# A two-block transformer kernel: top-k search one tile earlier, second block's weight split moved, last results in banks of their own

## The reference, cut to what matters

```python
# attention 1: 16 heads of 64, softmax over the 77 keys, then Wo, bo
x = x + tanh(g_xattn[1]) * attention1(layernorm(x), ctx)
# feed-forward 1: each expert chooses its tokens
n = layernorm(x)                                   # [4, 1024, 256]
affinity = softmax(n @ gate_w.T)                   # [4, 1024, 8]
gating, idx = top_k(affinity.transpose(0, 2, 1), 256)   # 256 tokens a batch and expert
h   = silu(n[idx] @ w_gate.T) * (n[idx] @ w_up.T)  # 1024 wide
x_e = h @ w_down.T
x = x + tanh(g_ffn[1]) * scatter_add(idx, gating * x_e)
```

## Time and profile before

| what | us |
|---|---|
| median of the runs shown | 1408.33 |
| the profiled execution | 1407.95 |
| its span (first to last instruction) | 1406.2 |
| PE busy in the span | 1297.4 (92%) |
| DVE, ACT, POOL busy | 911.0, 761.5, 627.0 |
| mean granted TensorE clock, of full speed | 0.945 |
| attention 1 | about 556 to 858 |
| feed-forward 1 | about 857 to 1406 |

### The profile page before, as it was taken

The page is one execution under the profiler, slowest core; times in us unless marked ns, Lnnn a source line. Parts: engine busy times, 40 slices in busy tenths (PEclk is TensorE's granted clock), DMA queues, the critical chain, the costliest instruction groups (busy, mean ns, idle before and its releaser), DMA issues.

```text
span 1406.2 us, 29217 instructions
## 1 busy us (share of the span) xinstructions
PE 1297.4 (92%) x9858; PEld 975.7 (69%) x9859; DVE 911.0 (65%) x2128; ACT 761.5 (54%) x2315; POOL 627.0 (45%) x664
## 2 busy tenths in 40 slices
PE   7966699999999999899999985899999999999997
PEld 3755588879999968788888773356656666566555
DVE  2887664565555577778776885777776555566651
ACT  3775332432332365988887752655645555555551
POOL 2177678666666540454444433133333333333113
PEclk8675599999999999999999996999999999999999
DMA  4657444654334351100210103244444444444322
GB/s 146 213 163 184 96 50 56 122 109 67 63 60 64 63 142 40 39 32 32 91 39 24 34 31 93 106 120 121 121 121 124 150 158 148 126 130 129 108 45 31
DMA packets 81546, 133.17 MB, mean 95 GB/s; under 512 B 24662, under 2 KB 71260, under 8 KB 76316
## 3 DMA queue, kind: packets, MB, share of 16 engines
q1 hardware_dynamic: 51132, 93.92, 20.1%
q0 software_dynamic: 29312, 37.57, 16.5%
q10 hardware_dynamic: 992, 0.27, 0.1%
HBM read 95.08 MB, written 36.65 MB: 94 GB/s over the span
## 4 chain that ended last, share of the span: by engine, by line
PE 70%; DVE 10%; DMA 6%; issue 5%; POOL 5%; ACT 2%; SPq 0%; POOLq 0%; ACTq 0%; DVEq 0%
PE psG L124 5%; PE psG L126 5%; PE psG L125 5%; PE psU L124 5%; PE psU L126 5%; PE psU L125 5%; PE psYb L124 4%; PE psYb L125 4%; PE psYb L126 4%; DMA stage<-in_w 3%; PE psP L1798 2%; PE psS L124 2%; PE psS L125 2%; PE psS L126 2%; PE psOL L126 2%
## 5 line engine op out<-in xcount | busy, mean ns | idle before, releaser
L2118 POOL DMA_INDIRECT out_x<-yo,gidx x64 | 100.2, 1566 | 324.0 <-ACT yo L2220 310.8
L2268 DVE SCALAR_TENSOR_TENSOR hid<-psU,sil 128x512 f32<-128x512 f32 x128 | 88.4, 691 | 167.2 <-ACT sil L2209 166.7
L980 POOL DMA_INDIRECT x_rows<-yo,tabs x78 | 124.7, 1599 | 91.7 <-ACT yo L1052 68.0
L1720 ACT ACTIVATE pr<-psS,mx 128x77 f32<-128x77 f32 x512 | 158.8, 359 | 5.2 <-DVE mx L1889 5.2
L2209 ACT ACTIVATE sil<-psG 128x512 f32<-128x512 f32 x128 | 76.4, 597 | 118.1 <-PE psU L126 118.1
L126 PE MATMUL psYb<-W1dh,hl 128*128 128x256 f16 x512 | 139.6, 273 | 0.0
L125 PE MATMUL psYb<-W1dl,hh 128*128 128x256 f16 x512 | 139.6, 273 | 0.0
L124 PE MATMUL psYb<-W1dh,hh 128*128 128x256 f16 x512 | 139.6, 273 | 0.0
L1079 DVE SCALAR_TENSOR_TENSOR hid<-psU,sil 128x512 f32<-128x512 f32 x78 | 53.8, 690 | 127.3 <-ACT sil L1043 127.2
L1720 ACT ACTIVATION_READ_ACCUMULATOR pr<-psS,mx 128x1 f32 x512 | 123.6, 242 | 0.0
L1043 ACT ACTIVATE sil<-psG 128x512 f32<-128x512 f32 x78 | 46.5, 596 | 134.2 <-PE psU L126 132.2
(11 more groups left out here) (407 smaller groups left out, 4331.1 us busy)
## 6 DMA issues: line engine op xcount, KB each, us to landing
w1u<-in_w SPq DMA_DIRECT2D x16, 2048.0 KB, 7.4
w1d<-in_w SPq DMA_DIRECT2D x16, 1024.0 KB, 9.7
stage<-in_w SPq DMA_DIRECT2D x8, 1536.0 KB, 8.9
X<-in_x SPq DMA_DIRECT2D x8, 512.0 KB, 8.6
n_rows<-xc SPq DMA_DIRECT2D x8, 512.0 KB, 9.0
x_rows<-X SPq DMA_DIRECT2D x8, 512.0 KB, 10.2
X<-x_rows SPq DMA_DIRECT2D x8, 512.0 KB, 8.0
out_x<-X SPq DMA_DIRECT2D x32, 128.0 KB, 1.7
```

The costliest lines, as they stand in the source:

```text
L980: pool.indirect_dma_start(x1_rows[:, :], bass.IndirectOffsetOnAxis(tabs[:, j, n, 0:1], 0), yo[:, par, n, :], None, compute_op=ALU.add).the ...
L1720: ins = act.activation(pr1[:, par, h * LK:(h + 1) * LK], psS1[:, q, i * LK:(i + 1) * LK], ACT.Exp, bias=mx1[:, h:h + 1], scale=1.0 / (SX * ...
L2118: pool.indirect_dma_start(out_rows[:, :], bass.IndirectOffsetOnAxis(gidx[:, half, col:col + 1], 0), yo1[:, j % 2, n, :], None, compute_op= ...
L2268: dve.scalar_tensor_tensor(hid1[:, f % 2, :], psU1[f % 2][:], SH / (SX * SW), sil1[:, f % 2, :], ALU.mult, ALU.mult).then_inc(d_hid, 1)
```

## The change

1. The first half's search stands one tile earlier: softmax at t == 18 (soft_max no longer ahead of that step's residual, but after probs_low0), rows at 22 to 24, digits from 26, THR in scores0 of tile 31, RANKS on PE in step 32 instead of 34 and in bank 3 of psS1 (so it needs exps1 of the last tile only).
2. The one-hot halves of the first half (4 on DVE) are placed singly between the last tiles' probs and statistics. The other two, the product with the token number, go to ACT as eight Copies with a scale (`values_act`), and FILL waits for them. TURN on PE stands before the last tile's transposes.
3. Block 1's up weights are split behind attention 1, in topk_scalar and topk_vector (eight pieces each), no longer in block 0's step.
4. The second half's row transposes stand in block 0's up (after f = 1 to 4), its first count at f = 7, and so do block 1's transposes (after f = 3), rows_high (f = 5) and rows_low (f = 6). The transposes signal for each k. gates_sync(1) goes behind load_down(1) on SP.
5. The pieces of the up weights are split in the order 0, 2, 4, 6, 1, 3, 5, 7, and `up` waits for four pieces at f = 0 and for the rest at f = 4.
6. The last block's four results go to four banks (two of psYb, two of psXb), each signalled and copied singly.

```diff
+        UP_PIECES = (0, 2, 4, 6, 1, 3, 5, 7)
-        drain0, drain1 = psS1[:, 0, :], psS1[:, 1, :]
-        FIRST_DIGIT = 27
-        ROWS_AT = ((0, 23), (1, 24), (0, 24), (1, 25))
-        FIRST_ODD = 25
-        TAIL_PE = {(27, "a"): THR, (28, "a"): RANKS, (29, "b"): FILL, (30, "b"): TURN}
-        TAIL_DVE = {(27, "a"): THR, (28, "b"): RANKS, (29, "b"): FILL, (30, "b"): TURN}
+        drain0, drain1 = psS1[:, 0, :], psS1[:, 3, :]
+        FIRST_DIGIT = 26
+        ROWS_AT = ((0, 22), (1, 23), (0, 23), (1, 24))
+        FIRST_ODD = 24
+        HOT = TURN + 1
+        TAIL_PE = {(26, "b"): RANKS, (29, "b"): FILL, (29, "d"): TURN}
+        TAIL_DVE = {(27, "a"): (RANKS,), (27, "d"): (HOT,), (27, "b"): (HOT + 1,), (28, "c"): (HOT + 2,),
+                    (28, "a"): (HOT + 3,), (29, "b"): (FILL,), (30, "b"): (TURN,)}
...
+            if t == FIRST_DIGIT + DIGITS // 2:
+                return THR
...
+        PE_ORDER = [("transposes_out", 5), ("turn2", 3), ("tail_a", 6), ("outputs0", 3), ("tail_c", 6), ("transposes_in", 0), ("scores0", 1),
+                    ("outputs1", 3), ("turn0", 2), ("outputs2", 3), ("turn1", 2), ("digit_odd", 3), ("scores1", 0), ("tail_b", 6), ("logits", 6), ("tail_d", 6)]
+        ACT_ORDER = [("exps1", 2), ("probs_high0", 3), ("shares_exp", 5), ("exps0", 2), ("probs_high1", 3), ("values", 5), ("copy_out", 5),
+                     ("high_in", 0), ("weights_high", 0), ("shares_copy", 5), ("probs_high2", 3)]
+        DVE_ORDER = [("stats_in", 0), ("normalise_out", 6), ("tail_c", 7), ("moments_in", 0), ("residual", 5), ("digit_odd", 5), ("probs_low0", 4), ("shares_max", 5),
+                     ("count_odd", 5), ("tail_a", 7), ("stats_out", 5), ("moments_out", 5), ("largest1", 2), ("reciprocals", 3), ("probs_low1", 4),
+                     ("maxima1", 2), ("low_in", 1), ("tail_d", 7), ("probs_low2", 4), ("largest0", 2), ("digit", 2), ("maxima0", 2),
+                     ("shares_div", 5), ("count", 2), ("normalise_in", 0), ("tables", 0), ("weights_low", 2), ("tail_b", 7)]
...
+        def values_act(act):
+            for half in range(2):
+                act.wait_ge(k_dve, D_MASK + 4 + 3 + half)
+                for i in range(half * (NI // 2), (half + 1) * (NI // 2)):
+                    row = hotC[:, i * RB:(i + 1) * RB, :]
+                    ins = act.activation(row, row, ACT.Copy, scale=tokv[:, i:i + 1])
+                ins.then_inc(k_act, 1)
...
         def topk_scalar(act):
+            for f in range(FT1 // 2):
+                second_high(act, f)
             soft_exp(act, 1)
             copies_act(act, 1)
-            for n in range(ROWS):
-                rows_act(act, 1, n, psYb[:, n, :].rearrange("p (k n) -> p k n", k=2))
-            gates_act(act, 1)
+            for f in range(FT1 // 2, FT1):
+                second_high(act, f)
...
             soft_div(dve, second, 1)
-            count(dve, second, 1, 0)
+            for f in range(FT1):
+                cols = slice(UP_PIECES[f] * UC, (UP_PIECES[f] + 1) * UC)
+                dve.wait_ge(d_wh, FT1 + f + 1)
+                dve.scalar_tensor_tensor(W1ul[1][:, cols], w1u[:, cols], SW, W1uh[1][:, cols],
+                                         ALU.mult, ALU.subtract).then_inc(d_wl, 1)
...
                 load_down(sp, j)
+                if j == 1:
+                    gates_sync(sp, 1)
...
                 pe.wait_ge(d_xl, KD * j + KD)
-                pe.wait_ge(d_wl, FT1 * j + FT1)
                 for f in range(FT1):
+                    if f % (FT1 // 2) == 0:
+                        pe.wait_ge(d_wl, FT1 * j + FT1 // 2 + f)
...
+                    if j == 0 and 1 <= f < 1 + ROWS:
+                        rows_pe(pe, 1, f - 1, [psYb[:, f - 1, k * P:(k + 1) * P] for k in range(2)])
+                    if j == 0 and f == 3:
+                        transposes(1, 1)
...
+        def result(j, n):
+            if j == NB1 - 1:
+                return (psYb[:, 0, :], psYb[:, 2, :], psXb[:, 0, 0:D], psXb[:, 1, 0:D])[n]
+            return psYb[:, n, :]
...
-            pipeline(pe, NB1, DD, [(2, up), (1, transposes), (3, down)], unroll=4, straight=True)
+            pipeline(pe, NB1, DD, [(2, up), (1, next_transposes), (3, down)], unroll=4, straight=True)
```

More of the change, by code:

```diff
@@ L1807, in run @@
                         wait(pe, c_res, t)
+                    if n == 0 and t == 19:
+                        pe.wait_ge(k_dve, 1)
                     if t == 0 and n == 2:
@@ L1819, in run @@
                         return
-                    for n in range(2):
-                        pe.wait_ge(c_exp[n], T)
+                    pe.wait_ge(c_exp[1], T)
+                    if TAIL_PE[t, name] != RANKS:
+                        pe.wait_ge(c_exp[0], T)
                     choose_pe(pe, 0, TAIL_PE[t, name], drain0, drain1)
@@ L1931, in counts @@
                     count(dve, ch, 0, 0)
-                if even_of(t) is not None:
+                if even_of(t) is not None and even_of(t) != THR:
                     count(dve, ch, 0, even_of(t) + 1)
@@ L1946, in run @@
                         return
-                    p = TAIL_DVE[t, name]
-                    choose_dve(dve, ch, 0, p, drain0, drain1)
-                    if p == RANKS:
-                        for n in range(6):
-                            one_hot_half(dve, ch, n)
+                    for p in TAIL_DVE[t, name]:
+                        if p >= HOT:
+                            one_hot_half(dve, ch, p - HOT)
+                        else:
+                            choose_dve(dve, ch, 0, p, drain0, drain1)
                 return run
@@ L2124, in ffn1_tensor, with next_transposes @@
         def ffn1_tensor(pe):
+            def next_transposes(j, ph):
+                if j != 1:
+                    transposes(j, ph)
             def transposes(j, ph):
@@ L2178, in run @@
                     par = ph % 2
-                    if isinstance(j, int) and j == 0:
+                    if j < 2:
                         return
@@ L2229, in hidden_high, with first_step, run, next_rows @@
                 return run
+            def first_step(f):
+                def run(j, ph):
+                    n = {2: 0, 3: 1, 4: 2, 6: 3}.get(f)
+                    if j == 0 and n is not None:
+                        rows_act(act, 1, n, psYb[:, n, :].rearrange("p (k n) -> p k n", k=2))
+                    if j == 0 and f == 5:
+                        rows_high(1, 1)
+                    if j == 0 and f == 7:
+                        gates_act(act, 1)
+                return run
+            def next_rows(j, ph):
+                if j != 1:
+                    rows_high(j, ph)
             work = [(2, silu(0)), (1, up_high(0)), (2, down_high(0))]
             for f in range(1, FT1):
-                work += [(2, silu(f)), (2, hidden_high(f - 1)), (1, up_high(f)), (2, down_high(f))]
-            work += [(2, hidden_high(FT1 - 1)), (1, rows_high)]
+                work += [(2, silu(f)), (2, hidden_high(f - 1)), (1, up_high(f)), (2, down_high(f)), (2, first_step(f))]
+            work += [(2, hidden_high(FT1 - 1)), (1, next_rows)]
             pipeline(act, NB1, DD, work + [(3, results)], unroll=4, straight=True)
```

115 lines of the change are left out of this document (65 added, 50 removed).

## The result

The changed kernel takes 1397.47 us (median of four runs, 1394.96 to 1399.40); the kernel before, run beside it, 1408.84 (1406.64 to 1411.07). The ratio is 0.9917, 95% interval 0.9901 to 0.9933: by it 11.7 us faster (9.4 to 13.9; the two medians as they stand differ by 11.4). The forecast was 1395.9 with a range of 1391.5 to 1401.5.

The account below looks back on a forecast made before the run. PE was taken as full in the steady blocks, so only its waits (attention 1's drain, between blocks 0 and 1, in block 1) could shrink: -8.0 - 2.8 - 1.3 = -12.1 from 1407.95 gives 1395.9 us, range 1391.5 to 1401.5.

Parts of the forecast that it names:

- Search a tile earlier: Attention 1's last tiles: a digit step moved earlier costs about +0.9 us, regained next step; taken as 0, bounds -1 to +1.
- One-hot halves singly: Drain of attention 1: last residual no longer behind the halves, -5.9 us, and -0.7 for THR; bounds -7.5 to -3.5.
- rival 1: Drain of attention 1: one-hot halves and pn shut each other out, last outputs 2 us later, 1397.9 us; chance 0.14.
- Residual to gather: Last residual to first gather: faster FILL (-0.9) and TURN no longer behind waiting transposes (-0.5), together -1.4 us, bounds 0 to -2.
- Gather to up(0): First gather to block 0's up: 11.26 us as before, with the same slow clock; no gain.
- Rows, transposes and splits inside up(0): From up(0) to up(1): 24.3 us instead of 27.1, so -2.8 us, bounds -3.2 to -1.
- Block 1's first three f: Start of block 1: its down weights bind, PE still waits 1.4 us; -1.3 us, bounds -2.7 and +4.3.
- Split behind attention hides: After attention 1: block 1's split, 4.9 us on DVE, ends some 2 us before rows_low(0); up to +3 if uncovered.
- Last results in own banks: Kernel end: block 14's scatter landing and four POOL scatters set the pace; 0, bounds -0.5 to +0.3 us.
- Rival 2: Block 1: down weights take 10.6 us, as behind a w1u; +5.6 and 1.7 for the clock, 1403.2 us; chance 0.10.
- Rival 3: Drain of attention 1: not DVE's alone, only half of the 8.0 us up to the gather comes, 1399.9 us; chance 0.11.
- Rival 4: Block 0: TensorE stays at 1.2 GHz throughout, +19 us gives 1415, slower than before; chance 0.03.

Follow-up runs that it names:

- e9: Changed kernel with digit numbers in PSUM, looser waits of the last scatters, block 0's down pieces by two, softmax at tile 19; ratio to the kernel before 0.9875.
- e4: Changed kernel with the two digit numbers that the one-hot halves compare in PSUM instead of SBUF; 1393.32 us, ratio to the kernel before 0.9895.
- e3: Changed kernel with the last block's results in pairs again, as before the change; ratio to the kernel before 0.9935.
- e5: Changed kernel with block 2's up weights loaded only when block 1's down weights are, so the loads pair again; 1410.57 us, ratio to the kernel before 0.9988.
- e11: Changed kernel with block 1's up weights split inside block 0's step again, all else kept; ratio to the kernel before 0.9979.
- e2: Kernel before with only parts 3 to 6 of the change, the old drain of attention 1 kept; 1404.95 us, ratio to the kernel before 0.9962.
- e10: Changed kernel with up weights split in plain order and up waiting for all eight pieces; ratio to the kernel before 0.9935.
- e1: Kernel before with only parts 1 and 2 of the change, feed-forward 1 as before; 1405.15 us, ratio to the kernel before 0.9964.

## Why the prediction was right, and where its terms were wrong

- **What bounds the kernel.** Right: the time came from the places where PE waited, and the steady blocks gave nothing (478.92 and 478.91 us).
- **Search a tile earlier, taken as 0.** It cost 1.00, the upper bound. The residual of tile 28 comes 2.29 us late (243.65 for 241.36), and tile 29's step gives only 1.29 of it back (7.94 for 9.23). The step with the softmax takes 11.05 us in place of 10.19; with the softmax back at tile 19, e9 is 0.64 faster.
- **One-hot halves singly: 6.6 forecast, 3.73 measured.** This is the step that failed. Of the missing 2.9, 1.00 is the search's, as above; behind tile 29 the drain gave 4.73. The working let the four halves stand in time in which DVE waited, and left pn at its 1.91. The halves did stand there, but the one beside pn stretched it, and PE's outputs of the last tile went back with it. e4 gives 1.64 back by removing just this: from tile 29 to the last residual it takes 14.21 us, a gain of 6.39 of the 6.6; 0.2 stay unexplained. So the 6.6 were worked out rightly but for pn. It is rival 1, priced at 2 us and given 0.14. It should have been in the sum: the row of a normalise taking 2.00 beside pn was there. Two of the prediction's own signs of being wrong came with it or behind it: pn and a half of over 1.5 us, and an end of down(15) to end of the kernel that is shorter than before (9.5 us for 10.4).
- **Residual to gather: 1.4 forecast, 2.37 measured.** Right in kind, too small. FILL took 1.06 for 1.91 as worked out, but also started 0.61 sooner behind the residual, since the logits and transposes ahead of it ran at full clock too; and TURN, standing free, gave 0.90 and not 0.5. The gather came at a distance of 272.44, 1.9 behind the 270.5 that the forecast's 8.0 makes of 278.54.
- **Gather to up(0), taken as 0: 0.41 gained.** PE's wait for the split rows fell from 2.08 to 1.41. It is not shown to be the change's: with the same code there, e3 to e9 took 10.86 to 11.39 us, beside 10.85 after and 11.26 before.
- **Rows, transposes and splits inside up(0): 2.8 forecast, 2.05 measured.** The work of up(0) came out as worked out, 24.1 us (25.07 less the wait) for 24.3, with the clock back at the same point as before. What was missed is the 0.96 us for which PE still waits for gxl ahead of up(1).
- **Block 1's first three f: 1.3 forecast, 2.41 measured.** The chain was right link by link. From up(0)'s end (886.19 - 0.96 = 885.23) to the issue of w1d 2.46 us (forecast 2.5), to its landing 4.9 (5.0), from ACT's first down piece at 892.64 to PE 1.68 (1.7): 9.09 for 9.2. The surplus only mirrors the term above: up(1) started 0.96 late, into a wait that the weights set anyway, which shrank from the 1.4 of the forecast to 0.19. The two terms together: 4.1 forecast, 4.46 measured. e5 and e11 show the same chain with a longer load, and from up(0) to the fourth f 6.8 and 7.7 us lost.
- **Split behind attention hides.** Right: DVE's eight pieces run from 854.05 for 5.04 us, and e2 has no delay at up(0). They end 0.43 us ahead of rows_low(0), where the forecast had some 2 to spare.
- **Order of the pieces: 0.** Right in the steady blocks (e10).
- **Last results in own banks: 0 forecast, 0.73 measured.** The step "the chain there is block 14's scatter landing, then four scatters" was true of that one execution and incomplete: the pair's result on ACT was a second bound at the same moment, with 0.30 of idle in front that looked like issue. With faster landings it binds alone (4.70 us in e1, 4.05 in e3). As 0.72 of the 0.73 is the difference of the two landings (5.00 and 4.28), the gain needed a faster landing and own banks together.
- **Rival 2** was real, if priced too low (8.8 us in e5 for 7.3), but did not occur: its condition, a w1u on the queue with w1d, was gone. **Rival 3**, half of the 8.0 up to the gather, did not come: 6.10 did, and what is missing at the residual has rival 1's reason and the search's. **Rival 4**, a clock that stays down through block 0, was refuted: in up(0) it was back within some 6 us in the worst case.

The forecast hit the time because 2.9 missing at the residual and 0.75 in up(0) were met by 1.0, 0.4, 1.1 and 0.9 behind them, 0.2 short of the sum. That the errors cancelled was luck in the drain's part; for the two terms of blocks 0 and 1 it follows from the chain. There was luck in the execution too: its clock stayed full after pn's wait, where it fell in four of six.

## What to carry to other kernels

When an instruction is moved into idle time of its own engine, look at what the neighbours run there: two engines that both read SBUF can cost each other most of what the idle time gives (of 2.0 us, 0.35 was left here), and moving one operand to PSUM undid that. When a buffer comes free earlier, the worth lies often in the load that follows it: 4.9 to 5.6 us for the down weights with nothing ahead of them, 11.2 behind a load of twice the size. Where a queue seems to set the pace, look also at what else releases its rows: a bound that falls on the same moment shows no idle time, and takes over once the first gets faster.

## What was not expected of the hardware

- The same wait of 3.16 to 3.17 us on TensorE cost nothing in two executions, some 1.1 us in one and 2.2 us in three. A kernel with such a wait has a time that spreads by that much; shortening it to 1.30 us took this spread away in four of four, one execution each.
- The second one-hot half and pn took 2.48 and 2.67 us, where each takes 1.21 and 1.91 undisturbed. The starts and ends fit engines that exclude each other for a whole instruction: pn late by the first half, the second half by pn, pn's small parts by the second half.
- TensorE's clock was full again 3 to 6 us after up(0)'s first matmul, by the execution, with the same instructions: up to 1.5 us of difference.
- The landing that the last scatters wait for took 3.99 to 5.00 us behind the same four scatters of block 14, by the execution.
